# The node numbers in PSUM as bfloat16 packed in words: a graph attention stage on one core

## The reference, cut to what matters

```python
h = (x_flat @ W_gat).reshape(M, HEADS, NUM_EXPERTS)          # 4 heads, 4 values each
e = leaky_relu(a_src[src] + a_dst[dst], negative_slope=0.2)
e_max = segment_max(e, dst, num_segments=M)
ee = exp(e - e_max[dst])
denom = segment_sum(ee, dst, num_segments=M)
msg = h[src] * (ee / (denom[dst] + 1e-16))[:, :, None]
agg = segment_sum(msg, dst, num_segments=M)
```

## Time and profile before

| | us |
|---|---|
| median of three runs | 1598.56 |
| lowest, highest | 1596.64, 1599.18 |
| profiled execution: span from the first to the last instruction | 1598.4 |
| DVE busy in it | 1248.3 |
| POOL busy in it | 876.9 |
| PE busy in it | 869.5 |

### The profile page before, as it was taken

One profiled execution on the slowest core, in us unless ns is written; L12 is line 12 of the kernel. 1 busy time (PEld: TensorE's weight loads), 2 busy tenths in 40 slices (PEclk: granted clock), 3 DMA queues, 4 the chain that ended last, 5 costly groups with the idle time before them and its releaser, 6 DMA issues.

```text
span 1598.4 us, 36932 instructions
## 1 busy us (share of the span) xinstructions
PE 869.5 (54%) x13361; PEld 683.8 (43%) x13361; DVE 1248.3 (78%) x2794; ACT 451.1 (28%) x813; POOL 876.9 (55%) x891
## 2 busy tenths in 40 slices
PE   0323233248888862554488884666666665553340
PEld 0223222237777752554133332555555555543340
DVE  6998898876667644996999986677777667788878
ACT  0232242224444433773133330212211121121120
POOL 0045665546666660000577777777777777777700
PEclk9999855556766655776699995555555555555555
DMA  7000000022222216100310110111111111111101
GB/s 166 7 20 21 27 28 27 29 56 50 51 49 49 50 51 95 42 28 12 29 10 10 10 10 10 12 12 12 12 14 12 13 12 12 12 12 24 23 2 26
DMA packets 113952, 45.80 MB, mean 29 GB/s; under 512 B 92631, under 2 KB 108799, under 8 KB 113538
## 3 DMA queue, kind: packets, MB, share of 16 engines
q1 hardware_dynamic: 84098, 22.43, 7.3%
q0 software_dynamic: 27632, 19.12, 7.0%
q10 hardware_dynamic: 2064, 2.10, 0.7%
HBM read 28.17 MB, written 15.93 MB: 28 GB/s over the span
## 4 chain that ended last, share of the span: by engine, by line
DVE 36%; issue 8%; PE 8%; DVEq 1%; ACT 0%; ACTq 0%
DVE edges_work L1950 7%; PE edges_acc L2460 3%; DVE edges_hotT L1950 3%; PE edges_acc L2449 2%; DVE all_stack L2195 1%; DVE graph_left L1823 1%; DVE graph_left L1821 1%; DVE all_eo L1992 1%; DVE all_sums L2211 1%; DVE edges_left L1821 1%; DVE edges_left L1823 1%; DVE graph_left L2274 1%; DVE edges_high L2244 1%; DVE all_sums L2271 1%; DVE edges_term_parts L1820 1%
## 5 line engine op out<-in xcount | busy, mean ns | idle before, releaser
L336 POOL DMA_INDIRECT edges_rows<-table,edges_src x576 | 563.0, 978 | 175.5 <-issue 174.9
L192 DVE TENSOR_TENSOR sorting_keys<-sorting_keys 128x512 f32<-128x512 f32 (+2 forms) x370 | 209.8, 608 | 16.6 <-ACT sorting_keys L317 13.2
L723 POOL DMA_INDIRECT x_rows<-mixture_sent,mixture_slot x128 | 144.3, 1128 | 127.5 <-DVE mixture_slot L785 89.0
L728 POOL DMA_INDIRECT y_rows<-mixture_yt,mixture_xin x144 | 156.2, 1085 | 103.6 <-ACT mixture_yt L950 79.4
L2508 ACT ACTIVATE edges_hotT<-edges_h 128x1024 bf16<-128x1024 bf16 x72 | 69.8, 1021 | 326.1 <-PE edges_h L2403 326.1
L1063 PE MATMUL mixture_bank<-mixture_xT,sorting_w_part 128*128 128x128 bf16 x864 | 111.9, 260 | 30.7 <-ACT mixture_xT L936 14.3
L1063 PEld LDWEIGHTS mixture_bank<-mixture_xT,sorting_w_part 128*128 x864 | 86.9, 107 | 57.4 <-issue 45.4
L1950 DVE TENSOR_TENSOR edges_work<-edges_feats,all_eo 128x2048 bf16<-128x2048 f32 x48 | 109.3, 2277 | 0.2 <-DVE all_eo L2003 0.2
L2460 PE MATMUL edges_acc<-edges_term_parts,edges_work 128*128 128x20 bf16 x1728 | 51.6, 179 | 100.6 <-DVE edges_term_parts L1824 100.6
L2460 PEld LDWEIGHTS edges_acc<-edges_term_parts,edges_work 128*128 128x128 bf16 x1728 | 49.1, 104 | 108.1 <-issue 108.1
L2403 PE MATMUL edges_h<-edges_ident,edges_work 128*128 128x128 bf16 x576 | 67.2, 310 | 31.7 <-DVE edges_work L1950 31.7
(11 more groups left out here) (477 smaller groups left out, 2170.0 us busy)
## 6 DMA issues: line engine op xcount, KB each, us to landing
edges_rows<-table,edges_src POOLq DMA_INDIRECT x576, 2.4
mixture_xin<-x_rows SPq DMA_DIRECT2D x144, 49.0 KB, 1.8
all_eo<-y_rows SPq DMA_DIRECT2D x16, 256.0 KB, 3.9
y_rows<-mixture_yt,mixture_xin POOLq DMA_INDIRECT x144, 2.6
sorting_w<-in_L_ffn_w_dram SPq DMA_DIRECT2D x4, 512.0 KB, 8.4
x_rows<-mixture_sent,mixture_slot POOLq DMA_INDIRECT x128, 2.3
out_dram<-all_x_sb SPq DMA_DIRECT2D x8, 256.0 KB
constants_src_i<-in_L_ffn_edge_index_dram SPq DMA_DIRECT2D x1, 1024.0 KB, 5.2
```

Source lines behind the costliest of these rows:

```text
L192: self.st.mark(dve.tensor_tensor(target[half], source[0], source[1], (ALU.min, ALU.max)[half]))
L336: pool.indirect_dma_start(to, None, rows, where).then_inc(done, 16)
L723: pool.indirect_dma_start(x_rows, bass.IndirectOffsetOnAxis(ap=slot[g % 2][:, c, t:t + 1], axis=0), now[c][:, t, :], None).then_inc(scatte ...
L728: pool.indirect_dma_start(y_rows, bass.IndirectOffsetOnAxis(ap=xin[j % XB][:, ROWX - 2:ROWX - 1].bitcast(U32), axis=0), yt[j % YB][:, :], ...
```

## The change

The node numbers are seen as bfloat16 in the same PSUM bank, so they take 64 words of it and not 128. They are written as words: the 128 bfloat16 numbers in SBUF (`node16`) are read as 64 words and copied to 64 words of PSUM. Everything that reads `node_ps` (`equal_to` for every 0/1 matrix, and two comparisons in the strays, lines 2054 and 2055) reads bfloat16 from then on. Nothing else is different: the order, the semaphores and the other operands stay.

```diff
@@ -1709,7 +1709,7 @@
         h1 = a.ps("h1", [H, 2, G])
         acc = a.ps("acc", [P, 2, G])
         back = a.ps("back", [P, 4, K * C])
-        node_ps, keys_ps = feats[:, 0, :], feats[:, 1, :]
+        node_ps, keys_ps = feats[:, 0, :].bitcast(BF16)[:, 0:P], feats[:, 1, :]
@@ -1979,7 +1979,7 @@
             st.link(dve.tensor_copy(node16[:, :], node_i[:, :]))
-            st.mark(dve.tensor_copy(node_ps[:, 0:P], node16[:, :]))
+            st.mark(dve.tensor_copy(feats[:, 0, 0:P // 2], node16[:, :].bitcast(F32)))
             st.link(dve.tensor_copy(ad_left[:, :, :], ad_sb[:, :, :]))
```

## The result

| | before, us | after, us |
|---|---|---|
| median (4 runs each) | 1597.68 | 1569.19 |
| lowest, highest | 1596.64, 1599.18 | 1567.32, 1570.94 |
| span of the profiled execution | 1598.4 | 1569.1 |
| DVE busy | 1248.3 | 1131.7 |

The ratio of the times is 0.982, with a 95% interval from 0.9806 to 0.9833: 28.5 us less, 1.8%. The forecast was 1568.5 us, range 1561 to 1580. DVE lost 116.6 us of work, four times what the time fell by; where the rest went is the subject of this part.

What follows compares the result with a forecast made beforehand. DVE sets the dense stage's pace, PE close behind; POOL's gathers form a second chain. DVE's gains (23.7 us, then 0.64 us per group) are capped by the last gather at 30.0 us: 1568.5 us, range 1561 to 1580.

Steps and rivals of the forecast that it cites:

- Price of the comparison: All 136 comparisons: 16-bit operands go two at a time, 2277 to 1210 ns for 2048 elements, 677 ns for 1024.
- Dense stage: Before the laps: PE's own pace limits the gain to 1.15 us per token group; 23.7 us by the laps' start.
- Laps: Each lap group gains 0.64 us, as PE's 48 matmuls then end last and a 0.43 us wait appears at line 2255.
- the late counts: Two serial places, line 1950: a pair of comparisons, then matmuls; 2 x 1.6 = 3.2 us less.
- the first pair: Start of the dense stage: the first pair of comparisons is ready 1.6 us sooner.
- Gathers: POOL's unchanged gathers make DVE wait some 12.6 us at line 1917, 3 us at 2219; gain at most 30.0 us.
- Tail: From line 2219 of the last group to the end: 51.5 us without comparisons, unchanged.
- The base of the sum: Whole kernel: profiled span 1598.4 less 30.0 us, with 0.2 us between span and median, gives 1568.5 us.
- One element a cycle from PSUM: Rival for all comparisons: PSUM keeps the rate, they stay at 2277 and 1210 ns, time 1598.5 us; chance 0.12.
- POOL shut out: Rival: the faster comparison stretches gathers beside it, 0.8 us for each of 85, time 1636 us; chance 0.04.
- Gathers that do not hold DVE: Rival: neither wait for gathers appears, DVE's own chain gives 46.1 us, time 1552 us; chance 0.04 with other gains.

Runs made afterwards that it cites:

- the run with broken pairs: Kernel after, but the comparison's second operand read with innermost step 0 instead of two stored copies; 1600.46 us in a single execution.
- the laps' half: Kernel after, but the dense stage and late counts read float32 node numbers, only the laps' comparisons the packed bfloat16 ones; 1577.63 us, ratio 0.9880.
- the second profiled execution: Kernel after, unchanged, measured again with five executions on the same chip as two other runs; 1568.32 us, ratio 0.9819.
- the SBUF run: Kernel after, but all 0/1 matrices read the bfloat16 node numbers from SBUF (node16) and not from PSUM; 1613.77 us, ratio 1.0098.
- the eight extra gathers: Eight more gathers ahead of POOL's first gather of rows; 1578.60 us on the kernel after, 1597.65 us on the kernel before (ratio 0.9997).
- the dense half: Kernel after, but the laps' comparisons read float32 node numbers, the dense stage and late counts the packed bfloat16 ones; 1574.40 us, ratio 0.9859.

## Why the prediction was right

**Price of the comparison.** Forecast 1210 and 677 ns from slope and fixed part of the earlier trace rows; measured 1215 and 681. That the operand in PSUM allows the fast form was a choice between two values that no row before could decide, and it came out. The tier table of the Trainium skill's page VectorE: DVE Perf Modes gives `tensor_tensor` with any PSUM operand one element a cycle; here the measurement differs, 1215 ns for 2048 elements where one a cycle takes 2277. The condition of its page Vector Engine (DVE) Microarchitecture Reference, 5.1 (2-byte types, innermost step 1), fits both the change and the run with broken pairs.

**Dense stage.** 9.97 us forecast for a token group, 9.92 measured; 23.7 us in all at the start of the laps with the first matrix, measured 226.5 - 201.3 = 25.2 at the first line 2219, counted from the first gather. Most of the 1.5 us too few lie in the stage: at its last bias addition DVE is 20.7 us ahead (184.5 against 163.9), where 19.4 were forecast. A token group gains 1.20 and not 1.15 us; where the rest lies was not followed up.

**Laps.** 0.64 us a group forecast. At line 2219 of group 20 DVE was 36.8 us ahead (511.6 against 474.8), forecast 36.5. That this is so close is partly luck: the dense stage gave 1.5 us more than forecast, and the first 20 groups gained 0.58 us each and not 0.64. Neither bears on the end, since the gathers take the surplus at line 1917. The prediction also said that with nothing but the late counts and the first pair won in the dense stage 28.3 us would be reached; by the laps' half it would have been nearer to 27 (an estimate: 22.2 us measured there, and 4.8 for the first pair and the late counts). The wait at line 2255 was forecast at 0.43 and is 0.46 us in the group shown.

**Gathers.** Waits of 12.6 and about 3 us were forecast at lines 1917 and 2219, 13.0 and 5.7 us appeared (11.8 and 3.7 in the second profiled execution). The gain that is left at the last group is the term on which the time hangs: forecast 30.0 us, measured 28.5 us in the profiled execution and 29.9 in the second one (772.0 against 742.1). In the first the last gather starts 2.4 us later than before, counted from the first one, of which a median of 947 ns after 944 makes 1.7 us over 575 gathers; line 2219 then follows 2.6 us behind it, where 3.4 were forecast. In the second the last gather starts at 738.5, exactly as before, and line 2219 follows after 3.6 us. The forecast took the gathers' pace as fixed, and it is, within 2.4 us.

**Tail.** 51.5 us forecast after line 2219 of the last group, 50.4 measured. DVE's next read of PE's third product used to wait for it by 1.2 us; while DVE waited for the rows, PE finished it. In the runs in which DVE does not wait for rows at the last group (the two halves, for example) that wait of 1.2 us is still there, and so are 51.5 us. This I had missed; it has the sign opposite to the slower gathers.

**The base of the sum.** 1568.5 us is the median of the three runs before, 1598.56, less 30.0. A fourth run puts that median at 1597.68, and the same gain would then lead to 1567.7 us. The distance of 0.7 us from 1569.19 is therefore in part luck; the gain, 28.5 us where 30.0 were forecast, is the fairer measure. The 0.2 us that the sum puts between span and median is no property of an execution either: where both are on record, a run takes about 1.8 us more than its span (1570.94 and 1569.1 for the kernel after). So the profiled execution before took about 1600.2 us (an estimate), 2.5 us above the median, and was a rather long one.

**The rivals.** One element a cycle from PSUM: ruled out by the duration. POOL shut out: the mechanism is real, and the SBUF run shows it at 44.6 us, but it goes by the number of SBUF inputs, and the change keeps that at one. Gathers that do not hold DVE: ruled out by the two DMA waits and by the eight extra gathers.

What stays open: why the laps' half alone gained 0.56 us per group after group 20 and not 0.67. No run was made for it. The timelines say only where: the group from line 2219 of group 33 to that of group 34 took 17.88 us before and 17.93 us with the laps' half, and the dense half, whose laps have the old comparisons, lost 0.67 us in the same group.

## What to carry to other kernels

When one engine is made faster, write down for every stream that it meets when that stream arrives, in absolute times of the trace; the gain ends at the smallest lead, here 30 us of 117 us of saved work. A wait that appears is not a gain to be had before the next limit behind it is known: 13 us of waiting taken away gave about 2. And where GpSimd issues gathers beside VectorE, count the SBUF inputs of VectorE's instructions: the routing's gate, an operand of 64 words, was worth 4 us when it moved to PSUM, and the node numbers, another of 64 words, cost 45 us when they moved to SBUF.

## What the runs showed of the hardware

- A comparison with a bfloat16 operand in PSUM, a bfloat16 one in SBUF and a bfloat16 output took 1215 to 1217 ns for 2048 elements, and with both operands in SBUF 1218 to 1219 ns. With the innermost step 0 in the second operand it took 2283 ns.
- In the laps a gather's instruction on POOL that started beside a comparison with one SBUF input took 0.94 to 0.96 us, and beside a comparison of the same length with two 1.67 us in the median and 1.86 us at most. Beside a float32 product of 2.29 us it took 2.82 us with two SBUF inputs and 0.94 us with one.
- A copy of 128 bfloat16 numbers as 64 words into PSUM took 228 ns, after 0.29 us for 128 converted ones.
